# Six layer norms of a cross-attention stack: by chunks and token halves, parameters loaded once, one norm moved between MLP blocks

## The reference, cut to what matters

```python
x = x + alpha * single_head_attention(x, ctx)
for i in (1, 2):
    h = layer_norm(x) * ln_scale_i + ln_offset_i
    q, k, v = h @ wq + bq, ctx @ wk + bk, ctx @ wv + bv      # 16 heads of 128, plus bias_k, bias_v as key and value 362
    x = x + softmax(q k^T / sqrt(128)) v @ wo + bo
h = layer_norm(x) * ln_mlp_scale + ln_mlp_offset
x = x + gelu(h @ w_fc1 + b_fc1) @ w_fc2 + b_fc2
```

## Time and profile before

| | us |
|---|---|
| median of 2 runs (2073.85 to 2075.85) | 2074.85 |
| the profiled execution: its own time | 2076.53 |
| its span, first to last instruction | 2074.7 |
| PE busy | 1846.5 (89%) |
| DVE busy | 1160.0 (56%) |
| ACT busy | 805.5 (39%) |
| POOL busy | 771.5 (37%) |
| mean granted TensorE clock | 0.968 |

### The profile page before, as it was taken

The page is one execution under the profiler, slowest core; times in us unless marked ns, Lnnn a source line. Parts: engine busy times, 40 slices in busy tenths (PEclk is TensorE's granted clock), DMA queues, the critical chain, the costliest instruction groups (busy, mean ns, idle before and its releaser), DMA issues.

```text
span 2074.7 us, 29971 instructions
## 1 busy us (share of the span) xinstructions
PE 1846.5 (89%) x11204; PEld 1750.3 (84%) x11204; DVE 1160.0 (56%) x2525; ACT 805.5 (39%) x1832; POOL 771.5 (37%) x634
## 2 busy tenths in 40 slices
PE   8775999999869999998795999999986999999879
PEld 4664998998859999998795899998885999998879
DVE  3654555555455555555677555555545555555465
ACT  4423433434324334334364443433323433333344
POOL 3464144342143342430375424244134143342144
PEclk9987999999989999999898999999998999999999
DMA  8742011111021111110271102011012011110022
GB/s 246 201 129 56 21 47 51 42 48 30 11 57 42 42 51 31 53 36 10 86 222 57 52 22 61 27 47 52 16 41 54 20 52 45 42 52 26 21 97 88
DMA packets 74051, 123.77 MB, mean 60 GB/s; under 512 B 14352, under 2 KB 26000, under 8 KB 73908
## 3 DMA queue, kind: packets, MB, share of 16 engines
q1 hardware_dynamic: 71604, 117.66, 19.7%
q10 hardware_dynamic: 2304, 4.20, 0.7%
HBM read 119.22 MB, written 2.61 MB: 59 GB/s over the span
## 4 chain that ended last, share of the span: by engine, by line
PE 73%; DVE 15%; ACT 5%; issue 3%; POOL 2%; DMA 2%; SPq 0%; ACTq 0%; DVEq 0%; POOLq 0%
PE psum L510 24%; PE psum L512 22%; PE psum L511 22%; PE psum L723 3%; DVE stats L1352 1%; PE psum L533 1%; DVE a_lo L1121 1%; DVE a_lo L1126 1%; DVE prob L1361 1%; ACT prob L994 1%; DVE xT L1337 1%; POOL wbuf_lo L445 1%; DVE g_lo L1117 1%; DVE pT_lo L1117 1%; DVE xT L1460 1%
## 5 line engine op out<-in xcount | busy, mean ns | idle before, releaser
L399 POOL TENSOR_TENSOR wbuf_hi<-stage,zero_col 128x512 fp32r<-128x512 f32 x256 | 266.5, 1041 | 1109.3 <-PE psum L512 624.7
L510 PE MATMUL psum<-pT_hi,ctx_rows_hi 121*128 121x250 f32 (+3 forms) x1152 | 336.1, 292 | 4.1 <-DVE pT_lo L1117 4.1
L445 POOL TENSOR_TENSOR wbuf_lo<-stage,wbuf_hi 128x512 fp32r<-128x512 f32 x256 | 329.1, 1285 | 20.0
L512 PE MATMUL psum<-pT_hi,ctx_rows_lo 121*128 121x250 f32 (+3 forms) x1152 | 335.4, 291 | 0.0
L511 PE MATMUL psum<-pT_lo,ctx_rows_hi 121*128 121x250 f32 (+3 forms) x1152 | 334.4, 290 | 0.0
L510 PE MATMUL psum<-a_hi,wbuf_hi 128*128 128x400 f32 x720 | 264.6, 368 | 54.6 <-DVE xT L1337 20.5
L510 PE MATMUL psum<-ctxT_hi,a_hi 128*125 128x362 f32 (+1 forms) x832 | 280.7, 337 | 4.8 <-DVE a_lo L1126 4.8
L512 PE MATMUL psum<-ctxT_hi,a_lo 128*125 128x362 f32 (+1 forms) x832 | 273.1, 328 | 0.0
L511 PE MATMUL psum<-ctxT_lo,a_hi 128*125 128x362 f32 (+1 forms) x832 | 272.8, 328 | 0.0
L1117 DVE TENSOR_TENSOR a_lo<-psum,a_hi 128x500 fp32r<-128x500 f32 (+2 forms) x288 | 146.2, 526 | 220.4 <-ACT a_hi L817 219.8
L511 PE MATMUL psum<-a_lo,wbuf_hi 128*128 128x400 f32 x720 | 247.9, 344 | 0.0
(11 more groups left out here) (168 smaller groups left out, 3628.8 us busy)
## 6 DMA issues: line engine op xcount, KB each, us to landing
stage<-head_w_dram SPq DMA_DIRECT2D x256, 256.0 KB, 2.6
mlp_stage<-mlp_w_dram SPq DMA_DIRECT2D x32, 512.0 KB, 3.8
ctx_rows_in<-ctx_dram SPq DMA_DIRECT2D x12, 726.0 KB
ctxT_in<-ctxT_dram SPq DMA_DIRECT2D x12, 724.0 KB, 11.3
key_stage<-head_w_dram SPq DMA_DIRECT2D x32, 256.0 KB, 4.2
l0w<-l_w_dram ACTq DMA_DIRECT2D x16, 256.0 KB, 13.9
kb<-diff_scratch SPq DMA_DIRECT2D x32, 64.0 KB, 3.6
out_dram<-y_out SPq DMA_DIRECT2D x8, 200.0 KB, 2.0
```

The lines of the kernel that those rows point to most:

```text
L399: return nc.gpsimd.tensor_tensor(out, in_, zero_col[0:in_.shape[0], :].broadcast_to(tuple(in_.shape)), ALU.add)
L445: nc.gpsimd.tensor_tensor(lo, held, hi.bitcast(F32), ALU.subtract).then_inc(stage_free, 1)
L510: pe.matmul(out, a_h, x_hi, start=start, stop=False)
L512: return pe.matmul(out, a_l, x_hi, start=False, stop=stop)
```

## The change

1. All norm parameters are loaded once, at the start, into `norm_p` of three sets. `load_norm` is gone.
2. `x_ready`, `block_done` and the wait for the whole `h_lo` are gone. Means are summed chunk by chunk as the last output's adds finish; centring, squares, scaling, high and low parts are one instruction per chunk of 200 columns with a semaphore count each. The two multiplications become one instruction (scale and reciprocal deviation).
3. The first products (q0, bias row, q1 of a layer; hidden 0 and 1 of the MLP) run by token halves: 12 matmuls of 200 columns for piece 0, then for piece 1, each chunk after its own `n_lo`. Order: q0, s0, q1 of piece 0, then of piece 1.
4. The output biases are added with the first add of a block (`add(..., first)`), not by 4 instructions of their own.
5. The norm of half 1 layer 0 (`BETWEEN`) is done inside the MLP of half 0: means after block 9 (PE), centring after 10 (DVE), squares after 11 (ACT), variances and roots after 12 (PE, ACT, with a load of the sqrt table and back), scaling after 13 (DVE, before the low part of gelu 15), low parts of piece 0 after the adds of block 14. `x_next` is loaded at block 3.
6. ACT loads the next function's table after `h_hi`, not between roots and `h_hi`. The first MLP weights are split before the norm, the first four layer weights as their buffers come free.
7. In the single-head part the last key sums and `key_parts` come before the norm: DVE does 4 key sums after groups 4, 5 and 6 instead of 3, and all 32 by the last residual; SP loads keys 22 to 24 before its wait for the first half's outputs.

```diff
-            def norm_sums(k2):
+            def mean_sums(j, x, added):
+                for c in range(DC):
+                    added(c)
+                    for n in range(2):
+                        mm = pe.matmul(mean_of(j, n), mean_w[:, :], x[:, c, piece(n)], start=(c == 0), stop=(c == DC - 1))
...
+            def square_sums(j):
                 for n in range(2):
                     for c in range(DC):
+                        pe.wait_ge(n_sq, n_chunks(j, n, c))
+                        mm = pe.matmul(var_of(j, n), mean_w[:, :], sq[:, n, c, :], start=(c == 0), stop=(c == DC - 1))
                     mm.then_inc(n_var, 1)
...
             def layer(half, l):
-                pe.wait_ge(x_ready, x_is(half, l))
-                norm_sums(norm_at(half, l))
-                pe.wait_ge(n_lo, norm_at(half, l) + 2)
+                if j != BETWEEN:
+                        mean_sums(j, xT, lambda c: pe.wait_ge(y_done, (ph - 1) * R_LAYER + R_AT["o", H - 1] + c + 1))
+                    square_sums(j)
...
-                run_pieces("start")
+                for n in range(2):
+                    first_queries(0, n)
+                    bias_scores(n)
+                    first_queries(1, n)
+                run_pieces("start", 2)
...
             def mlp_block(half):                                  # PE
+                for n in range(2):
+                    for fb in range(2):
+                        first_hidden(fb, n)
                 for fb in range(FB):
-                    if fb + 1 < FB:
+                    if 0 < fb < FB - 1:
                         hidden(fb + 1)
...
+                    if again and fb == MEAN_AFTER:
+                        pe.wait_ge(xn_ld, 16)
+                        mean_sums(BETWEEN, x_next, lambda c: None)
+                    if again and fb == SQUARES_AFTER:
+                        square_sums(BETWEEN)
...
+                    if again and fb == SQUARED_AFTER:             # ACT
+                        norm_squares(BETWEEN)
+                    if again and fb == SQUARES_AFTER:
+                        load_table(ACT.Sqrt)
+                        norm_roots(BETWEEN)
+                        load_table(ACT.Gelu)
+                if again:
+                    act.wait_ge(g_mm, (half + 1) * FB)
+                    norm_hi(BETWEEN)
+                    load_table(ACT.Exp)
...
+            def norm_dve(j):
+                norm_centre(j, xT)
                 for n in range(2):
+                    norm_scale(j, n)      # reciprocal, 4 x (cen * scale * rstd)
+                    norm_lo(j, n)         # 4 x h_lo, each after its h_hi
...
+                    if again and fb == CENTRED_AFTER:             # DVE
+                        norm_centre(BETWEEN, x_next)
+                    if again and fb == SCALED_AFTER:
+                        norm_scale(BETWEEN, 0)
+                        norm_scale(BETWEEN, 1)
+                    if again and fb == FB - 2:
+                        norm_lo(BETWEEN, 0)
...
-            def load_norm(half, l):                               # SP
-                sp.wait_ge(x_ready, x_is(half, l))
-                sp.dma_start(norm_p[:, :, :], norm_d[l]).then_inc(norm_ld, 16)
...
                 elif ph > 0:                                      # POOL, split_weights, i < WBUFS
-                    pool.wait_ge(y_mm, ph * R_LAYER)
+                    user = ORDER[W_LAYER - WBUFS + i]
+                    pool.wait_ge(y_mm, (ph - 1) * R_LAYER + R_AT[user] + OUTPUTS[user[0]])
```

More of the change, by code:

```diff
@@ L83 @@
 CTX_ROWS_AT = (6, 8, 10, 12)
+MEAN_AFTER, CENTRED_AFTER, SQUARED_AFTER, SQUARES_AFTER, SCALED_AFTER = 9, 10, 11, 12, 13
 STAGES = 2
@@ L324, in _ @@
                 load_key_weights(9 + 2 * b)
-            for i in range(16, 22):
+            for i in range(16, 25):
                 load_key_weights(i)
@@ L328, in _ @@
             sp.dma_start(out_d[1], xT[:, :, :]).then_inc(landed, 16)
-            for i in range(22, LAYERS * H):
+            for i in range(25, LAYERS * H):
                 load_key_weights(i)
@@ L662, in weights, with bias_scores, first_queries @@
                     return w_hi[i % WBUFS], w_lo[i % WBUFS]
+                def bias_scores(n):
+                    if ph == 0:
+                        pe.wait_ge(w0_s, LAYERS)
+                    if j == BETWEEN:
+                        pe.wait_ge(m_add, (half * FB - 1) * DC + 1)
+                    first = slice(l * H, (l + 1) * H)
+                    product(bank[PT_BANK][0:H, piece(n)], lambda c: w0_hi[:, c, first], lambda c: w0_lo[:, c, first],
+                            **normed(j, n)).then_inc(s0_mm, 1)
+                def first_queries(h, n):
+                    hi, lo = weights("q", h)
+                    done = product(output("q", h)[:, piece(n)], lambda c: chunk(hi, c), lambda c: chunk(lo, c),
+                                   **normed(j, n))
+                    if n == 1:
+                        done.then_inc(y_mm, 1)
                 def queries(h):
@@ L1020, in attended_hi @@
                         kept.then_inc(u_hi, 1)
-                run_pieces("start")
+                queries_hi(0)
+                bias_row()
+                queries_hi(1)
+                wait(act, landed, half * (DC * 16) + 16)
+                run_pieces("start", 2)
                 act.wait_ge(rows_clear, 2)
@@ new lines, in norm_centre, with norm_scale @@
+                    dve.wait_ge(n_mean, n_pieces(j, n))
+                    for c in range(DC):
+                        nc.vector.tensor_tensor(cen[:, n, c, :], x[:, c, piece(n)], mean_of(j, n), sub).then_inc(n_cen, 1)
+            def norm_scale(j, n):
+                dve.wait_ge(n_sd, n_pieces(j, n))
+                nc.vector.reciprocal(rstd[:, n, :], rstd[:, n, :]).then_inc(n_rstd, 1)
+                dve.wait_ge(n_rstd, n_pieces(j, n))
+                for c in range(DC):
+                    scale = norm_p[:, j % (LAYERS + 1), c, SCALE_COL:SCALE_COL + 1]
+                    nc.vector.scalar_tensor_tensor(out=cen[:, n, c, :], in0=cen[:, n, c, :], scalar=scale, in1=rstd[:, n, :],
+                                                   op0=ALU.mult, op1=ALU.mult).then_inc(n_scaled, 1)
@@ new lines, in norm_lo @@
+            def norm_lo(j, n):
+                for c in range(DC):
+                    dve.wait_ge(n_hi, n_chunks(j, n, c))
+                    low_biased(h_lo[:, c, piece(n)], cen[:, n, c, :],
+                               norm_p[:, j % (LAYERS + 1), c, OFFSET_COL:OFFSET_COL + 1], h_hi[:, c, piece(n)])\
+                        .then_inc(n_lo, 1)
+            def norm_dve(j):
+                norm_centre(j, xT)
+                for n in range(2):
+                    norm_scale(j, n)
+                    norm_lo(j, n)
@@ L1299, in layer, with add @@
+            def add(out, value, x, l, m, first):
+                if first:
+                    bias = norm_p[:, l, m, RES_COL:RES_COL + 1]
+                    return nc.vector.scalar_tensor_tensor(out=out, in0=value, scalar=bias, in1=x, op0=ALU.add, op1=ALU.add)
+                return nc.vector.tensor_tensor(out, value, x, ALU.add)
             def layer(half, l):
                 ph = half * LAYERS + l
-                norm_dve(norm_at(half, l), half * 3 + l, last_keys if ph == 0 else lambda: None)
```

239 lines of the change are left out of this document (120 added, 119 removed).

## The result

The kernel with the change takes 2012.97 us (median of 2 runs) against 2074.85: a ratio of 0.970, 95% interval 0.966 to 0.974. The forecast was 2007 us with a range of 1985 to 2032. Its profiled execution took 2012.8 us, its span is 2011.0. The forecast's own sum, against the profiled execution of before, was 68.3 us; the trace gives 2076.5 - 2012.8 = 63.7.

A forecast was written before the change was run, and what follows sets the result against it. PE, busy 89% of the span, was taken as the bound, gains coming from its waits and slow clock around norms. Terms 18.4 + 13.1 + 7.0 + 11.7 + 12.0 + 6.1 = 68.3 us gave 2007 us, range 1985 to 2032.

The forecast's parts named there:

- The second norm, and the fifth: Layer 1 of halves 0 and 1: no parameter wait, chunk-wise chain; window 18.7 us, gains 13.1 and 12.0 us.
- The MLP norms: Third and sixth norms: shorter DVE work, gelu table load behind `h_hi`; window 17.3 us, gains 7.0 and 6.1 us.
- The first norm: Half 0, layer 0: parameter wait gone, key sums earlier; products end at 24.4 us instead of 42.8, gain 18.4 us.
- the last key should come about when the last output does: First norm: three key-weight loads move ahead of SP's wait, for which POOL stood 6.67 us.
- The moved norm: Fourth norm, into the MLP of half 0: 35.3 - 7.7 - 15.9 = 11.7 us gained, bounds 0 and 19.
- the collision with POOL: Moved norm: each of 8 DVE scalings may lose one POOL split, 0 to 8 us in all, 5 taken.
- the squares: Moved norm, on ACT after block 11: they wait for centring, gelu 12 queues behind; +2 us.
- the moved norm pays nothing: Rival, MLP of half 0: queues in blocks 10 to 15 take all its 11.7 us; 2019 us, chance 0.11.
- Other edits, at nothing: Output biases in the first add, earlier row to DRAM, earlier weight buffers: no gain; failed cover costs 2 to 4 us a norm.
- The clock stays up: Rival: PE never falls after 2.5 us pauses, 2 to 2.4 us more in four or five norms; 1997 us, chance 0.15.
- Only the late load goes: Rival: chunk hand-overs cost what pipelining gains, 39.3 us remain; 2036 us, chance 0.08 including the change not doing as said.
- The slow short matmuls: Rival: 384 products of 200 columns lose the single pass, 0.28 us more each; 2114 us, chance 0.03.

The follow-up runs named there:

- e5: Changed kernel with the store of the second half's x issued from ScalarE's queue instead of SyncE's: 2011.3 us, ratio 0.9685 to before.
- e6: Changed kernel with 13 unused mean matmuls filling TensorE's wait after the variance sums of the five unmoved norms: 2011.5 us, ratio 0.9683 to before.
- e8: Changed kernel with 7 unused mean matmuls filling TensorE's wait after the variance sums of the five unmoved norms: 2005.7 us, ratio 0.9653 to before.
- e1: Changed kernel with the moved norm put back behind the MLP block, in its new form by chunks and token halves: 2012.7 us, ratio 0.9687 to before.
- e10: Changed kernel with no norm moved, seven filler matmuls in all six norms, x store on ScalarE's queue, first norm's third split held: 2003.1 us, ratio 0.9637.
- e2: Kernel before the change, with only the norm parameters loaded once at the start and kept: 2052.6 us, ratio 0.9875 to before.
- e9: Changed kernel with seven fillers, x store on ScalarE's queue, moved norm respread with splits held, first norm's third split held: 2002.0 us, ratio 0.9632.
- after_again: The changed kernel, unchanged, timed and profiled a second time beside the other runs: 2013.1 us, ratio 0.9693 to before.
- e11: Changed kernel with seven fillers, x store on ScalarE's queue, moved norm respread with splits held, first norm's splits not held: 1999.3 us, ratio 0.9621.
- e4: Changed kernel with POOL's first four weight splits of the second half's first layer held until the moved norm is scaled: 2010.4 us, ratio 0.9676.

## Why the prediction was right, step by step

- **The second norm, and the fifth.** The forecast had the first `h_lo` at 9.05 us after the last product (579.76 - 570.81 = 8.95 to the product that waits for it) and the end at 18.7 (18.2). DVE's own chain is what is late next, as said, and the slow clock came. Inside, two sizes were off and nearly met. I took 200 columns for 0.167 us cold and 0.10 warm, by the slope over the columns. Products with 128 columns of weights run 0.213 cold and 0.112 warm; those with 16 columns (the bias scores) 0.167 and 0.092. With the same moving columns only the weight columns differ, so it is they that slow the wide ones, at either level of the clock. But only about 19 products ran cold, not the 36 of the first half, so the whole took 9.2 us for 9.6. The Trainium skill ("TensorE: Matmul & The Clock Gate", section "LDWEIGHTS (loading the stationary operand)") had warned of it: the estimate of 107 ns worked out from it is near the 112 measured at 2.4 GHz. At 1.2 GHz the rows show 213, and there the measurement decides.
- **The MLP norms.** 7.0 and 6.1 forecast, 7.5 and 5.0 found. The third had part of its products cold and the sixth all of its first half (granted clock 0.90 and 0.81): the clock is the difference. In the second profile of the kernel the two changed places (17.9 and 16.8 us), so which of them is longer is chance.
- **The first norm.** 2.4 us short. 0.8 of it is in the window (25.2 for 24.4), where "the last key should come about when the last output does" failed: the last output product ends at 143.2 us, and the residual that closes it stands behind a key sum until 146.1. e5 shows that the load named in the forecast was one of two waits, the store's landing being the other. The other 1.6 us is that the window begins later than before, which need not be the change: runs with the same single-head part begin it from 2.3 us earlier to 2.0 later than this one.
- **The moved norm.** 11.7 forecast, 11.8 found, and from the first output product to the last the MLP grew from 73.3 to 89.2 us, the 15.9 of the sum. Of its pieces the collision with POOL held (8.2 us for eight scalings instead of 2.9, 5.4 where I had taken 5). Two others missed and nearly cancel, which is luck: the squares were to cost 2 us, and the wait behind them is 0.65 us where such a wait was 1.61 before; and behind the 9.50 us wait PE ran the last block's products at the lower clock, 0.33 us apart, some 1.5 us that the sum has no term for. In the second profile of the kernel the gain is 9.4 us, in e5, e6 and e8, which leave this stretch alone, about 12. What the forecast did not see is that these 11.8 us are the norm's new form and not its place. A norm left in its place takes 18.2 us and a copy ahead of it; I had both numbers and did not compare them. e1 and e10 show it. The rival "the moved norm pays nothing" was right about the move and wrong about the time.
- **Other edits, at nothing.** Nearly so: the layers kept their length but for 0.8 to 2.4 us in the first one, where a weight lands late.
- **The rivals.** "The clock stays up" did not happen by itself; e8 shows its size: 4.4 to 4.7 us in five norms and not 10. Only some 19 short products ran slowly in the second norm, not 36, which is 1.2 us, and in the MLP norms PE then waits 1.24 us for `h_lo`. "Only the late load goes" is wrong in its own price too (e2: 25 us). The slow short matmuls did not come. Two small slips of the working: its upper bounds add to 93 us, not 92, and the price of the two table loads by its own figures is 2.5 us, not 2.4; in the trace each of the two loads takes 1.28 us and the next instruction starts within 0.02 us.

By part, from the runs: 25 us for the load, 13 for the token halves, nothing for the move; the remaining 24 or so of the 62 belong to the chunk-wise chain, the fused scaling, the order of the first norm and the earlier splits, which were not separated; the parts need not add, as e9 shows.

## What to carry to other kernels

Take the time that an engine waits for a transfer as an upper bound of what an earlier transfer gives, not as the gain: here 39 us of waits were worth 25, in part since the work behind them met another engine sooner. Before moving a step into another stage, price it in its improved form in its old place. And where TensorE waits 2 us or so in front of short matmuls, look at the granted clock behind the wait: matmuls with no use that fill it exactly took 1.2 us off the second and the fifth norm here, while too many gave nothing. One such place is left in every kernel of this document: near the end of each layer PE waits 2.66 us for `prob` (at 537 us of after), the clock is low behind it for some 3 to 7 us, and no run filled it.

## What the runs showed of the hardware

- Behind the waits of 2.59 us (3.71 in the first norm) TensorE ran at 1.2 GHz in all of the five norms, at once or after some products, for 3.3 us in the second and some 6.6 in the sixth; in the first it had fallen already behind a wait of 1.96 us. With the wait filled it stayed up in all five (e6) and in four of five (e8). After waits of 1.69 and 1.80 us at the same place of the program it stayed up once and fell once; behind one of 2.09 us it stayed up in after and fell in after_again; behind one of 2.77 us it fell in e9 and stayed up in e11.
- fp32r matmuls of 200 columns start 0.112 us apart with 128 weight columns and 0.092 with 16 at 2.4 GHz; 0.213 and 0.167 at 1.2 GHz. A plain fp32 matmul of 200 columns takes two passes of 0.18 us (26 records for 13 instructions).
- VectorE instructions with both operands in SBUF alternate with GpSimd's one for one while it has work: 128x200 took 1.0 us in the mean instead of 0.36 beside splits of 1.04 to 1.29 us. A multiplication with one tensor operand did so too (e2), a reciprocal did not. The Trainium skill ("SBUF — State Buffer", section "SBUF: two separate sides") describes a lock that is held for a whole instruction, and the trace agrees. With it, holding one side back moves the collision to whatever VectorE does next (e4, e9).
